# VectorE's share of the exponentials: a unit in all 17 chunks instead of 15, its passes split over two chunks, its values one block later

## What is computed

```python
qh = _split_heads(q @ Wq + bq)            # 16 heads of depth 8, 1024 queries
kh = _split_heads(k @ Wk + bk)            # 6404 keys
vh = _split_heads(v @ Wv + bv)
logits = jnp.einsum('bhsd,bhtd->bhst', qh, kh) / jnp.sqrt(DEPTH)
attn = jax.nn.softmax(logits, axis=-1)    # 16 * 1024 * 6404 exponentials
out = jnp.einsum('bhst,bhtd->bhsd', attn, vh)
```

## Time and profile before

| | |
|---|---|
| median of 3 timed executions | 799.97 us (799.95 to 800.89) |
| the profiled execution | 802.64 us, of which its span is 800.9 us |
| ACT busy | 723.6 us (90%) |
| PE busy | 696.5 us (87%) |
| DVE busy | 606.4 us (76%) |
| the attention's blocks | from 82 to 754 us of the span |

### The profile page before, as it was taken

The page is one execution under the profiler, slowest core; times in us unless marked ns, Lnnn a source line. Parts: engine busy times, 40 slices in busy tenths (PEclk is TensorE's granted clock), DMA queues, the critical chain, the costliest instruction groups (busy, mean ns, idle before and its releaser), DMA issues.

```text
span 800.9 us, 36509 instructions
## 1 busy us (share of the span) xinstructions
PE 696.5 (87%) x15090; PEld 313.6 (39%) x15090; DVE 606.4 (76%) x1712; ACT 723.6 (90%) x629; POOL 176.4 (22%) x318
## 2 busy tenths in 40 slices
PE   8996899999999899999998989998999999899841
PEld 4554244434443344334433443344434443444321
DVE  4568488858887788678867888588868886788666
ACT  3555799999999999999999999999999999999641
POOL 3436222212221222212211222122212221222100
PEclk8999699999999999999999999999999999999975
DMA  4354211111111111111111111111111111111000
GB/s 137 112 151 144 67 43 36 38 41 42 39 37 38 46 43 35 40 45 42 35 41 46 43 35 36 45 42 38 38 41 46 38 35 41 39 35 36 3 0 26
DMA packets 36991, 38.35 MB, mean 48 GB/s; under 512 B 8942, under 2 KB 35472, under 8 KB 36896
## 3 DMA queue, kind: packets, MB, share of 16 engines
q1 hardware_dynamic: 35788, 36.59, 15.9%
q10 hardware_dynamic: 1108, 0.46, 0.2%
HBM read 30.13 MB, written 6.42 MB: 46 GB/s over the span
## 4 chain that ended last, share of the span: by engine, by line
ACT 57%; issue 27%; PE 11%; DVE 3%; ACTq 1%; DMA 1%; POOL 0%; DVEq 0%; POOLq 0%
ACT probs L754 56%; PE ps L1296 2%; PE ps L1250 2%; PE ps L1258 1%; PE ps L1417 1%; PE ps L1287 1%; PE ps L1387 1%; ACTq L767 1%; DMA wq_sb<-in_L_xattn_Wq_dram 1%; PE ps L1241 0%; DVE probs L1185 0%; ACTq L752 0%; ACT ctx_t L667 0%; DVE stats L820 0%; PE ps L1493 0%
## 5 line engine op out<-in xcount | busy, mean ns | idle before, releaser
L754 ACT ACTIVATE probs<-ps 128x1536 f32<-128x1536 f32 (+1 forms) x536 | 669.5, 1393 | 7.6 <-PE ps L1387 7.6
L1417 PE MATMUL ps<-probs,v_op 64*9 64x512 f32 (+1 forms) x8256 | 524.4, 498 | 0.0
L1387 PE MATMUL ps<-q_op,k_op 59*32 59x512 bf16 x6432 | 335.9, 383 | 65.2 <-ACT probs L754 62.4
L1387 PEld LDWEIGHTS ps<-q_op,k_op 59*32 59x32 bf16 x6432 | 103.7, 90 | 350.9 <-issue 260.7
L1045 DVE TENSOR_SCALAR e_t<-ps 128x256 f32<-128x256 f32 x240 | 90.6, 419 | 145.4 <-PE ps L1387 145.4
L1417 PEld LDWEIGHTS ps<-probs,v_op 64*9 64x9 f32 x8256 | 172.6, 86 | 61.7 <-issue 5.7
L630 POOL TENSOR_SCALAR e_pow<-e_t 128x512 int32<-128x512 int16 x120 | 74.3, 620 | 357.8 <-DVE e_t L1045 357.8
L623 POOL COPY v_op<-v_all 128x108 f32<-128x108 f32 x136 | 64.3, 473 | 171.3 <-PE ps L1417 170.7
L1073 DVE SCALAR_TENSOR_TENSOR e_f<-e_f,e_pow 128x256 f32<-128x256 f32 x240 | 98.6, 449 | 0.0
L1062 DVE SCALAR_TENSOR_TENSOR e_u<-e_f 128x256 f32<-128x256 f32 x240 | 90.0, 415 | 0.2
L1067 DVE SCALAR_TENSOR_TENSOR e_f<-e_u,e_f 128x256 f32<-128x256 f32 x240 | 90.1, 416 | 0.0
(11 more groups left out here) (190 smaller groups left out, 243.1 us busy)
## 6 DMA issues: line engine op xcount, KB each, us to landing
k_op<-k_parts_dram SPq DMA_DIRECT2D x544, 36.0 KB
k_parts_dram<-k_parts SPq DMA_DIRECT2D x17, 288.0 KB, 2.9
k_op<-k_parts_dram SPq DMA_DIRECT2D x272, 12.0 KB
ctx_nat<-in_ctx_dram SPq DMA_DIRECT2D x16, 192.0 KB, 2.6
q_op<-q_parts_dram SPq DMA_DIRECT2D x32, 48.0 KB
q_parts_dram<-q_parts SPq DMA_DIRECT2D x2, 384.0 KB, 3.3
x_nat<-in_x_dram SPq DMA_DIRECT2D x1, 512.0 KB, 3.8
o_t<-att_rows SPq DMA_DIRECT2D x28, 16.0 KB
```

The source lines that it names most:

```text
L754: act.activation(probs[:, b % NP].rearrange("p u t -> p (u t)")[:, 0:columns], ps[:, bank:bank + BU, :].rearrange("p u t -> p (u t)")[:, 0 ...
L1387: return pe.matmul(ps[a:a + P // G, bank, :], k_op[W2 * r:W2 * r + KR, kslot, i, P * j + a:P * j + a + P // G], q_op[W2 * r:W2 * r + KR, q ...
L1417: last = pe.matmul(ps[32 * k:32 * k + DH + 1, ACC[h], a:b], v_op[W2 * h:W2 * h + W2, slot, j, (DH + 1) * k:(DH + 1) * (k + 1)], probs[W2 * ...
```

## The change

- `E_UNITS` goes from 15 to 17: chunks 1 and 16 have a shared block as well. ACT takes two banks of the third block in each chunk, and POOL makes `e_pow` in each.
- The passes of a unit are split. In chunk c DVE does the two bank passes of its unit (`take`), then the power and the product of the unit of chunk c-1, then `e_u` and the second `e_f` of unit c (`quadratic`, `cubic`). `e_f` and `e_pow` have two buffers, `e_u` one. At the ends of a phase the order differs: chunk 14 does the power of its own unit too, chunk 15 power and product of its own, chunk 16 the power; the product of unit 16 follows the take of the next phase's chunk 0. The turning of a phase's sums is spread over chunks 1, 2 and 3.
- PE waits for the bank passes only ahead of the third bank of the block that uses it again (semaphore `e_taken`), no longer ahead of the whole block.
- The values stand one block later: j = 2 of chunk c-2 behind s = 0 of chunk c, j = 0 of chunk c-1 behind s = 1, the halves of j = 1 behind s = 2 and s = 3. The wait for the product (`wait_e`) stands ahead of the first of these.
- Behind the loop stand the j = 2 values of chunk 15 and then those of chunk 16, the last of them with a wait for the last product.

The core of the diff:

```diff
-E_UNITS = NC - 2
+E_UNITS = NC
@@ PE, scores()
                 for u in range(BU - packed):
+                    if u == BU - 1 and taken is not None:
+                        taken()
@@ PE, chunk()
                 for s in range(LAST_BPC if c == NC - 1 else BPC):
-                    if s == 0 and c:
-
-                        wait(e_step, at(E_STEPS * (e_count(ph, c - 1) - 1) + E_TAKEN,
-                                        E_STEPS))
                     wait(probs_ready, at(f + s + 1, BPC))
-                    scores(m % KS, q, ph, c == NC - 1, s)
+                    shares = s == 0 if c else s == 1 and ph
+                    scores(m % KS, q, ph, c == NC - 1, s, taken_before if shares else None)
...
+                    elif s == 0:
+                        wait_e(ph, c - 2)
+                        values(1 - slot, f - 2 * BPC, 2, False)
+                    elif s == 1:
+                        values(slot, f - BPC, 0, False)
                     elif c == NC - 1:
...
-                    elif s == 0:
-                        values(slot, f - BPC, 0, False)
-                    elif s == 3:
-
-                        wait(e_probs, at(2 * e_count(ph, c - 1), 2))
-                        values(slot, f - BPC, 2, False)
+                        values(slot, f - BPC, 1, False, count=2)
                     else:
-                        values(slot, f - BPC, 1, False, a=(s - 1) * (HQ // 2), b=s * (HQ // 2))
+                        values(slot, f - BPC, 1, False, a=(s - 2) * (HQ // 2), b=(s - 1) * (HQ // 2))
@@ DVE
             for ph in range(PHASES):
-                take(ph, 0)
-                if ph:
-                    add_acc(ph - 1)
-                power(ph, 0)
...
-                for c in range(2, NC - 1):
+                for c in range(NC):
                     take(ph, c)
-                    power(ph, c)
+                    if c == 0:
+                        if ph:
+                            product(ph - 1, NC - 1)
+                        quadratic(ph, c)
+                        cubic(ph, c)
+                        if ph:
+                            add_acc(ph - 1)
+                        continue
+                    if c < NC - 2:
+                        power(ph, c - 1)
+                    if c < NC - 1:
+                        product(ph, c - 1)
+                    quadratic(ph, c)
+                    cubic(ph, c)
+                    if c == 1 and ph:
+                        turn_acc()
+                    elif c == 2 and ph:
+                        normalise_acc()
+                    elif c == 3 and ph:
+                        turn_rows(ph)
+                    elif c >= NC - 3:
+                        power(ph, c)
+                    if c == NC - 2:
+                        product(ph, c)
+            product(PHASES - 1, NC - 1)
```

More of the change, by code:

```diff
@@ L636, in _ @@
                     stage(m % 2, m, c * CT, ph % NG * G)
-                    if c != 1 and c < NC - 1:
-                        powers(ph, c)
+                    powers(ph, c)
         @block.scalar
@@ L1040, in take @@
                 bank = BU * (block % 2) + BU - 1
-                done = E_STEPS * (e_count(ph, c) - 1)
+                n, f, _ = place(ph, c)
                 dve.wait_ge(scores_done, block + 1 + AHEAD)
+                if n > 1:
+                    dve.wait_ge(e_pow_ready, n - 1)
                 for cols in halves:
@@ L1052, in take, with quadratic @@
                                              in1=e_low(e_t[:, cols]), op0=ALU.max, op1=ALU.subtract
+                                             ).then_inc(e_taken, 1)
+            def quadratic(ph, c):
+                n, f, done = place(ph, c)
+                for h, cols in enumerate(halves):
+                    dve.wait_ge(e_taken, E_TAKES * (n - 1) + 2 + h + 1)
+                    if n > 1:
+                        dve.wait_ge(e_probs, 2 * (n - 2) + h + 1)
+                    dve.scalar_tensor_tensor(out=e_u[:, cols], in0=f[:, cols], scalar=EXP2[0],
+                                             in1=f[:, cols], op0=ALU.add, op1=ALU.mult
+                                             ).then_inc(e_step, 1)
@@ L1053, in take, with cubic @@
+            def cubic(ph, c):
+                n, f, done = place(ph, c)
+                for h, cols in enumerate(halves):
+                    dve.wait_ge(e_step, done + h + 1)
+                    dve.scalar_tensor_tensor(out=f[:, cols], in0=e_u[:, cols], scalar=EXP2[2],
+                                             in1=f[:, cols], op0=ALU.add, op1=ALU.mult
                                              ).then_inc(e_step, 1)
             def power(ph, c):
-                block = ph * BPP + c * BPC + E_BLOCK
@@ new lines, in power, with product @@
+                for h, cols in enumerate(halves):
+                    dve.wait_ge(e_step, done + 2 + h + 1)
+                    dve.wait_ge(e_pow_ready, n)
+                    dve.scalar_tensor_tensor(out=f[:, cols], in0=f[:, cols], scalar=EXP2[3],
+                                             in1=e_pow[:, n % 2, cols].bitcast(F32), op0=ALU.add,
+                                             op1=ALU.mult).then_inc(e_step, 1)
+            def product(ph, c):
+                block = ph * BPP + c * BPC + E_BLOCK
+                n, f, done = place(ph, c)
+                for h, cols in enumerate(halves):
+                    dve.wait_ge(e_step, done + 4 + h + 1)
@@ L1499, in _ @@
             project_out(0)
+            pe.wait_ge(e_probs, 2 * (E_UNITS * PHASES - 1))
+            values((PHASES * NC - 2) % 2, BLOCKS - LAST_BPC - BPC, 2, False)
             pe.wait_ge(v_staged, PHASES * NC)
```

109 lines of the change are left out of this document (54 added, 55 removed).

## The result

The changed kernel takes 859.93 us (median of 5, 858.46 to 862.27) where the kernel before takes 800.69 (median of 5, 799.95 to 801.2): 1.075 times as long, with a 95% interval of 1.0734 to 1.0767. The forecast was 858 us. The profiled execution took 858.46 us, its span is 856.7.

The account below looks back on a forecast made before the run. ACT's own pace was taken to bound the kernel; 104 waits at 0.57 us (59.3), less 2.3 at seams, plus 1.3 at the end, give 58.3 us more, 858 us with the profile-to-median offset carried over; range 834 to 875.

Parts of the forecast that it names:

- What bounds, and ACT's pace: Middle of the attention: ACT's own pace is the time, 1.33 us a full block, 0.94 a shared one, 4.94 a chunk.
- The wait that decides: PE's queue behind the scores of s = 0: waits some 0.8 us a chunk for DVE's product of unit c-2.
- The price of one wait: Chunks 3 to 15: PE's lateness delays DVE's next take, making ACT's s = 1 0.57 us late in each chunk.
- The cheap end: Lowest price of one chunk's wait: 0.31 us, with no feeding back and a signal of 0.05.
- No feeding back: Rival: DVE still starts at 0.92, so each of 104 waits costs 0.35 us; 835 us, chance 0.12.
- The sum: Whole kernel: 59.3 - 2.3 + 1.3 = 58.3 us more, giving 858 us.
- The seams at chunk 16: Chunk 16's block gets shorter for ACT: 0.33 us gained at each of 7 seams, 2.3 us.
- The end: Behind ACT's last blocks: moved values (0.86 us) and DVE's last unit make the end 1.3 us later.
- The start: Half-clock stretch from 79.65 to 93.30, where PE is the limit: 0 us, from -0.5 to 1.
- Products in time: Rival: the product is done by 2.9, ACT keeps its pace, 4.1 us gained; 796 us, chance 0.05.
- DVE the bound: Rival: chunk 1's DVE list of 5.05 us against 4.94 eats the gain; about 800 us, chance 0.03.
- The falling clock: Rival: PE's clock halves, some 1.2 us more a chunk for a fourth of 136 chunks; 898 us, chance 0.05.

Follow-up runs that it names:

- The half values: Changed kernel with half j = 1 values behind s = 1 and s = 2, full j = 0 values behind s = 3, wait kept behind s = 0: 817.41 us.
- the kernel with the wait behind s = 1: Changed kernel with the full values of s = 0 and s = 1 exchanged, so PE's wait for the product stands behind s = 1: 795.86 us.
- the pass behind the cubic: Changed kernel with an idle 0.67 us DVE pass behind the cubic passes in chunks 2 to 14 of each phase: 859.05 us.
- a pass of 0.67 us more ahead of the product: Changed kernel with an idle DVE pass between bank passes and power, in chunks 2 to 14 of each phase: 962.67 us.
- the kernel with the values as before: Changed kernel with PE's values where they stood before the change (wait behind s = 3), DVE's order as changed: 1005.32 us.

## Why the prediction was right

**What bounds, and ACT's pace.** Right. ACT's blocks keep their length (5.05 us for four in a row with a shared one among them), and it is ACT's gaps that make the time.

**The wait that decides.** Right in place, engine and cause. The forecast said that PE waits some 0.8 us a chunk for DVE's product; the trace has 0.89, and the view of who waited for whom has this row for the stretch from 130 to 820 us (total us, times, longest):

```profile
PE ps L1466 <- DVE probs L1103: 89.1, 112, 0.9
```

Over the whole run it is 95.3 us in 119 waits. By their places these are the 13 x 8 = 104 of the forecast, in chunks 3 to 15 at mostly 0.89 us, 7 in chunk 2 at 0.25 and 8 in chunk 16 at 0.22. In chunks 2 and 16 no gap of ACT follows, as forecast. DVE's take stands 421.35 - 420.24 = 1.11 behind ACT's start of s = 1, where 1.14 was forecast and 0.92 had been.

**The price of one wait.** Forecast 5.51 us a chunk, measured 5.56. Three of its five terms were slightly off, and partly against each other: signal 0.15 for 0.10, the scores of s = 1 to those of s = 2 1.08 for 1.14, from there to the take 0.72 for 0.66. The product behind the take, 2.75, and values to scores, 0.86, were read right.

**The cheap end of it was wrong.** "No feeding back" (0.35 a wait, 835 us) was priced with the take held at 0.92 behind ACT's start. The half values took all the extra lateness away and gave 817. The forecast value did not hang on this, since with full values the loop is above that floor, but the lower bound did. Two slips of the forecast are small: the cheap end of a wait is 0.30 by its own terms (3.67 + 0.05 + 0.86 + 0.66 - 4.94), not 0.31, and its upper bound comes to 874, not 875.

**The sum.** ACT's first start to its last went from 82.1 and 752.2 to 78.8 and 807.1, that is from 670.1 to 728.3 us: 58.2 more, where 59.3 - 2.3 = 57.0 were forecast. It is closer than its parts. By ACT's starts the 13 chunks of a phase are each some 0.61 us longer and not 0.57, 63.0 us in all for 59.3. The seams at chunk 16 give back 2.6, chunks 1 and 2 of the later phases together 1.0, and chunk 1 of the first phase, for which nothing was set, another 1.3 (6.11 for 7.38). 63.0 - 2.6 - 1.0 - 1.3 = 58.1. So a part of the agreement is luck. The end, from ACT's last start to `add_acc`, went from 4.4 to 5.3: 0.9 to 1.0, where 1.3 was taken. Of the terms of that 1.3, the values moved (0.86) account for nearly all of it. What was added for DVE's last unit was too much: in the kernel with the wait behind s = 1, leaving that unit out changed nothing.

**The start.** ACT's first exponential is 3.3 us earlier in the profile after than in that of before. Nothing of the change stands ahead of it, and it lies between 78.8 and 80.7 us in the profiles of all kernels with the change, so it belongs to the single executions that were profiled: that of before lay 1.95 above its median, that of after 1.47 below. That is why the profiled executions differ by 55.8 us and the medians by 59.2. The forecast was carried over to the median, and that fits: 858 against 859.93.

**The rivals.** Products in time (796 us) did not happen. Its price came out in the kernel whose wait is moved one block on, 795.86, but not by its parts: there chunk 1 takes 5.24 us against 5.32 before, 0.08 less where 0.39 was priced, and more came from chunk 2 (4.94 for 5.09) and from chunk 1 of the first phase (6.16 for 7.38). DVE the bound: refuted by the pass behind the cubic. The falling clock: not in the changed kernel (1.00 throughout the middle), but with a pass of 0.67 us more ahead of the product it came 22 times, so it was a real danger. Its price, 1.2 us for a chunk at the half clock, was too low: there a fall cost 1.69.

## What to carry to other kernels

When work on one engine is put off to make room for something more urgent, look up where its consumer waits: the new wait must stand behind the moved work by the clock, not by the count of blocks, and the queue behind it tells what it costs. If the wait delays the very event that starts the producer, the two engines form a loop, and its length, summed from five or so rows of a timeline, was here the period as soon as it exceeded that of the bounding engine; two engines at 82% and 77% busy then set the time. The whole loss here went, and a small gain came in its place, when two groups of matmuls in PE's order changed places.

## What was not expected of the hardware

The granted clock of PE fell to 0.50 22 times within the attention of the kernel with a pass more ahead of the product (mean over the run 0.935, where the changed kernel has 0.976), where PE waited 1.56 us in each chunk of 6.23. It never fell in the middle of the changed kernel, where PE waited 0.89 in 5.56. But in the kernel with the values as before PE waits 1.61 us in each chunk of 6.69, and a stretch of 87 us there has the clock at 1.00 throughout:

```profile
418.00:505.00 87.00, 61.39 (x1468) 27.01 (x1456) 55.00 (x161) 65.94 (x53) 11.65 (x26) 1.00 0.11 31
505.60:509.00 3.40, 3.14 (x40) 1.24 (x48) 2.21 (x7) 0.67 (x2) 0.28 (x1) 0.50 0.17 51
```

Only behind it, in the second row, is the clock at 0.50. Falls come 9 times in this kernel's attention: once early, and once in each phase near its end. So a wait of that length does not bring a fall each time, and the busy share does not tell either: PE is busy for 61.39 of 87.00 us, 71%, through the stretch without a fall, and for 10.54 of 14.00 us, 75%, ahead of a fall in the other kernel. What tells them apart stays open.
